# W1 times a fused matrix by Strassen: four pairs of seven block products, in a chain of conditional LoRA layers on one core

## The reference

```python
x = x + einsum('bct,bcd->bdt', x, L0_weights[adapter])            # C = 64, D = 64
x = x + x @ L1_W + (x @ L1_A[adapter]) @ L1_B[adapter]            # rank 16, 16 adapters
x = x + x @ L2_W.T + (x @ L2_A[labeler]) @ L2_B.T * 0.5           # rank 32, 5 labelers
x = x + x @ L3_W.T + 2.0 * top-2-gated sum over 8 experts of rank 16
```

## Time and profile before

| | us |
|---|---|
| median of 3 runs | 543.56 (542.45 to 544.06) |
| the profiled execution, its own time | 544.38 |
| its span | 542.6 |

### The profile page before, as it was taken

How to read it: one execution, slowest core, us unless ns; L and a number is a source line. 1 busy time by engine, 2 the same in 40 slices (tenths; PEclk the granted TensorE clock), 3 DMA queues, 4 the chain that set the end, 5 groups by cost and what they waited for, 6 DMA issues and landing times.

```text
span 542.6 us, 9086 instructions
## 1 busy us (share of the span) xinstructions
PE 533.7 (98%) x2812; PEld 475.9 (88%) x2812; DVE 252.5 (47%) x609; ACT 162.8 (30%) x314; POOL 155.9 (29%) x247
## 2 busy tenths in 40 slices
PE   7999999999999999999999999999999999999996
PEld 6999999999999999999987788888888888888885
DVE  3842222132211111213987675664756647566463
ACT  4641312121110111113734332333323333233322
POOL 2501000000000000353653644434444344443400
PEclk9999999999999999999999999999999999999999
DMA  7803020035242111120050421323313233132312
GB/s 280 291 32 132 2 78 16 1 106 170 83 152 76 40 39 44 39 82 1 23 167 2 132 98 48 102 80 123 104 46 103 79 120 107 43 105 79 118 29 77
DMA packets 24060, 46.76 MB, mean 86 GB/s; under 512 B 7636, under 2 KB 13396, under 8 KB 23908
## 3 DMA queue, kind: packets, MB, share of 16 engines
q1 hardware_dynamic: 23844, 45.85, 25.4%
q0 software_dynamic: 192, 0.59, 0.3%
HBM read 33.39 MB, written 13.04 MB: 86 GB/s over the span
## 4 chain that ended last, share of the span: by engine, by line
PE 95%; DVE 2%; DMA 1%; SPq 0%; ACT 0%; issue 0%; POOL 0%; DVEq 0%
PE bank L1281 27%; PE bank L1315 25%; PE bank L1232 15%; PE bank L1301 8%; PE bank L1363 4%; PE bank L1371 4%; PE bank L1248 4%; PE bank L1379 3%; PE bank L1366 1%; PE bank L1365 1%; DMA w2raw<-in_w_dram 1%; PE bank L1325 1%; DVE t_lo L902 1%; PE bank L1342 0%; PE bank L1352 0%; PE bank L1331 0%
## 5 line engine op out<-in xcount | busy, mean ns | idle before, releaser
L1281 PE MATMUL bank<-e_lo,w1t_hi 128*128 128x488 f32 (+2 forms) x240 | 86.9, 362 | 0.0
L1281 PE MATMUL bank<-e_hi,w1t_hi 128*128 128x488 f32 (+2 forms) x240 | 86.8, 362 | 0.0
L1281 PE MATMUL bank<-e_hi,w1t_lo 128*128 128x488 f32 (+2 forms) x240 | 86.7, 361 | 0.0
L902 DVE TENSOR_TENSOR w1t_lo<-raw,w1t_hi 128x1024 fp32r<-128x1024 f32 x18 | 24.7, 1370 | 76.6 <-ACT w1t_hi L661 60.0
L1232 PE MATMUL bank<-g_hi,w2s_hi 128*128 128x384 f32 (+1 forms) x144 | 48.3, 336 | 0.3 <-DVE e_lo L902 0.3
L1281 PEld LDWEIGHTS bank<-e_lo,w1t_hi 128*128 128x128 f32 x240 | 45.2, 188 | 3.9
L1281 PEld LDWEIGHTS bank<-e_hi,w1t_hi 128*128 128x128 f32 x240 | 45.0, 188 | 4.0
L1281 PEld LDWEIGHTS bank<-e_hi,w1t_lo 128*128 128x128 f32 x240 | 45.1, 188 | 3.9
L1232 PE MATMUL bank<-g_lo,w2s_hi 128*128 128x384 f32 (+1 forms) x144 | 48.2, 335 | 0.0
L1232 PE MATMUL bank<-g_hi,w2s_lo 128*128 128x384 f32 (+1 forms) x144 | 48.2, 335 | 0.0
L902 DVE TENSOR_TENSOR e_lo<-bank,e_hi 128x384 fp32r<-128x384 f32 (+1 forms) x24 | 13.0, 558 | 60.7 <-ACT e_hi L696 60.7
(11 more groups left out here) (233 smaller groups left out, 1330.0 us busy)
## 6 DMA issues: line engine op xcount, KB each, us to landing
raw<-in_x_dram SPq DMA_DIRECT2D x16, 512.0 KB, 3.6
out_dram<-ost SPq DMA_DIRECT2D x32, 256.0 KB, 2.1
b1s<-b1scr SPq DMA_DIRECT2D x32, 217.5 KB, 2.7
raw<-in_b1w_dram SPq DMA_DIRECT2D x10, 512.0 KB, 3.3
w2raw<-in_w_dram SPq DMA_DIRECT2D x7, 512.0 KB, 8.0
graw<-in_w3a3wr_dram SPq DMA_DIRECT2D x4, 768.0 KB, 8.7
graw<-in_w3a3wr_dram SPq DMA_DIRECT2D x8, 196.0 KB, 7.5
b1scr<-b1stage_hi SPq DMA_DIRECT2D x8, 192.0 KB
```

The costliest lines, as they stand in the source:

```text
L902: V.tensor_tensor(dst, src, f32(hi), ALU.subtract).then_inc(signal, 1)
L1281: ins = nc.tensor.matmul(stage_bank(u, j)[:, 0:WIDTH[c]], W1T[u][a][:, k, :], EX[c][z][:, k, :], start=(k == 0 and (a, z) == TERMS[0]), st ...
```

## The change

The W1 rows are multiplied by E with Strassen's scheme (the form with seven products, the same that the x tiles use). Row tile j and row tile j + 4 make a pair. Per pair PE runs seven products of 12 matmuls of 512 columns (`rows_pair`), and two products with the 296 extra columns (`row_tables`, 24 matmuls each). The LoRA rows stay plain, in chunks of 512, 512 and 296 columns. The combinations of E's four quarters, e1 to e4, are whole 128x2048 tiles. Since E is kept as high and low parts only, each takes several passes: e1 three and e2 two on DVE, e3 three and e4 two on POOL, during the LoRA rows. Then ACT and DVE split them (`e_hi`, `e_lo`). The left combinations of each pair are POOL's (`row_sum`, 128x512). M's own combinations, formed by POOL row by row before, become four instructions of 128x1536 on POOL (`front_sum`) late in and after the last pair, and four of 128x512 on DVE (`back_sum`). Nearly every buffer moves.

The order on PE:

```diff
-            pe.wait_ge(s_a2l, 2)
-            for r in range(2 + LORA):
-                rows(r, r % 2)
-            with pe.Fori(1 + LORA // 2, ROWS // 2) as i:
-                rows(2 * i, 0)
-                rows(2 * i + 1, 1)
+            def row_tables(j, h):
+                e = 2 * j + h
+                above(pe, s_rxa, 2 * (e - 1))
+                left = XR if h else XA
+                pe.wait_ge(s_rl, OPS * j + OPERAND["xb" if h else "xa"])
+                for k in range(K):
+                    for a, z in TERMS:
+                        ins = nc.tensor.matmul(bank[RT + h][:, 0:EC], left[a][:, k, :], EM[z][:, k, EXT], ...)
+            def rows_pair(j):
+                ops = OPS * j
+                if j:
+                    pe.wait_ge(s_ra, 2 * j - 1)
+                else:
+                    pe.wait_ge(s_accl, ACC_A + 3)
+                row_product("p1")
+                pe.wait_ge(s_rl, ops + OPERAND["cs"])
...
+                row_product("p5")
+                pe.wait_ge(s_rl, ops + OPERAND["ds"])
...
+                row_product("p6")
+                row_tables(j, 1)
+                pe.wait_ge(s_rcp, 2 * j + 1)
+                row_product("p2")
+                pe.wait_ge(s_radd, 3 * j + 2)
+                pe.wait_ge(s_rl, ops + OPERAND["cs2"])
+                row_product("p7")
+                pe.wait_ge(s_rl, ops + OPERAND["xb2"])
+                row_product("p3")
+                pe.wait_ge(s_radd, 3 * j + 3)
...
+                row_product("p4")
+                if j < LASTR:
+                    row_tables(j + 1, 0)
+            pe.wait_ge(s_a2l, 1)
+            for r in range(LORA):
+                lora_rows(r)
+            row_tables(0, 0)
+            for j in range(NR):
+                rows_pair(j)
```

DVE's list from the end of stage 1:

```diff
+            w1_lo(1)
+            dve.wait_ge(s_accl, ACC_A - 1)
+            V.tensor_tensor(e1, e_part("b12", 0), e_part("b11", 0), ALU.subtract).then_inc(s_e1, 1)
+            dve.wait_ge(s_e1, 1)
+            V.tensor_tensor(e1, e1, e_part("b12", 1), ALU.add).then_inc(s_e1, 1)
+            dve.wait_ge(s_e1, 2)
+            V.tensor_tensor(e1, e1, e_part("b11", 1), ALU.subtract).then_inc(s_e1, 1)
+            identity_rows(0, 0)
+            identity_rows(0, 1)
+            lora_lo(0, 0)
+            dve.wait_ge(s_e1, 3)
+            V.tensor_tensor(e2, e_part("b22", 0), e1, ALU.subtract).then_inc(s_e2, 1)
+            lora_lo(0, 1)
+            dve.wait_ge(s_e2, 1)
+            V.tensor_tensor(e2, e2, e_part("b22", 1), ALU.add).then_inc(s_e2, 1)
+            lora_lo(0, 2)
+            dve.wait_ge(s_e2, 2)
+            e_lo(1)
+            row_lo(XA[1][:, :, :], raw[0][:, :, :], XA[0][:, :, :], OPERAND["xa"])
+            lora_lo(1, 0)
+            e_lo(3)
+            lora_lo(1, 1)
+            row_lo(CS[1], tmp[:, :, :], CS[0], OPERAND["cs"])
+            dve.wait_ge(s_e4, 1)
+            e_lo(2)
+            lora_lo(1, 2)
```

DVE in each pair, and with `j == LASTR` in the last one (`row_lo` splits a left operand):

```diff
+            def rows_pair_lo(j):
...
+                row_lo(DS[1], tmp[:, :, :], DS[0], ops + OPERAND["ds"])
+                row_lo(XR[1][:, :, :], raw[1][:, :, :], XR[0][:, :, :], ops + OPERAND["xb"])
+                if j == LASTR:
+                    split_lo("b11", FRONT)
...
+                V.tensor_tensor(bank[BB][:, :], bank[BB][:, :], held_p1[:, :], ALU.add).then_inc(s_radd, 1)
+                row_lo(CS[1], raw[1][:, 0:KH, :], CS[0], ops + OPERAND["cs2"])
...
+                V.tensor_tensor(bank[BD_][:, :], bank[BB][:, :], held_p5[:, :], ALU.add).then_inc(s_radd, 1)
+                row_lo(XR[1][:, 0:KH, :], tmp[:, :, :], XR[0][:, 0:KH, :], ops + OPERAND["xb2"])
...
+                if j == LASTR:
+                    split_lo("b12", FRONT)
+                    dve.wait_ge(s_s0h, 1)
+                    lo(S[1][:, :, 0:C3], TBC[:, :, :], S[0][:, :, 0:C3], s_s0l)
+                    split_lo("b21", FRONT)
+                dve.wait_ge(s_rw, made + PRODUCT["p7"])
+                V.tensor_tensor(m_row(j, "b22"), bank[BB][:, :], held_p5[:, :], ALU.add).then_inc(s_radd, 1)
```

DVE in the first pair of x tiles:

```diff
+                dve.wait_ge(s_ra, 2 * NR)
+                split_lo("b21", BACK)
+                split_lo("b22", FRONT)
+                dve.wait_ge(s_ml, SPLIT_LO["b12b"])
+                back_sum("t1")
+                split_lo("b22", BACK)
+                dve.wait_ge(s_tb, FORMED["t1"])
+                back_sum("t3")
+                plain_lo(CS[1], raw[1][:, 0:KH, :], CS[0], 2)
+                plain_lo(DS[1], raw[1][:, KH:K, :], DS[0], 3)
+                dve.wait_ge(s_ml, SPLIT_LO["b22b"])
+                dve.wait_ge(s_tb, FORMED["t3"])
+                back_sum("t2")
                 V.memset(f32(h1c[:, :]), 0.0).then_inc(s_z, 1)
+                dve.wait_ge(s_tb, FORMED["t2"])
+                back_sum("t4")
                 xn_lo(0, YB)
```

POOL's list from the end of stage 1:

```diff
+            e3, e4, e2 = (TF[n][:, :, :] for n in (2, 3, 1))
+            pool.wait_ge(s_accl, ACC_A - 1)
+            nc.gpsimd.tensor_tensor(e3, e_part("b22", 0), e_part("b12", 0), ALU.subtract).then_inc(s_e3, 1)
+            pool.wait_ge(s_e3, 1)
+            nc.gpsimd.tensor_tensor(e3, e3, e_part("b22", 1), ALU.add).then_inc(s_e3, 1)
+            pool.wait_ge(s_e3, 2)
+            nc.gpsimd.tensor_tensor(e3, e3, e_part("b12", 1), ALU.subtract).then_inc(s_e3, 1)
...
+            row_sum(0, "s1")
+            pool.wait_ge(s_e2, 2)
+            nc.gpsimd.tensor_tensor(e4, e_part("b21", 0), e2, ALU.subtract).then_inc(s_e4, 1)
+            pool.wait_ge(s_e4, 1)
+            nc.gpsimd.tensor_tensor(e4, e4, e_part("b21", 1), ALU.add).then_inc(s_e4, 1)
+            for j in range(NR):
+                if j:
+                    row_sum(j, "s1")
+                for which in ("s2", "s3", "s4"):
+                    row_sum(j, which)
...
+            front_sum("t1")
+            pool.wait_ge(s_tf, FORMED["t1"])
+            pool.wait_ge(s_ml, SPLIT_LO["b12f"])
+            front_sum("t3")
             pool.wait_ge(s_idx, 48)
+            pool.wait_ge(s_s0l, 1)
+            for s in range(2):
+                nc.gpsimd.memset(bdraw[s], 0.0).then_inc(s_bdz, 1)
+            pool.wait_ge(s_rxa, 4 * NR)
+            pool.wait_ge(s_a1, 16)
+            take(0, choose(0))
...
             pool.wait_ge(s_bdz, 2)
+            diagonal(0, 0, 0)
+            pool.wait_ge(s_tf, FORMED["t3"])
+            pool.wait_ge(s_ml, SPLIT_LO["b22f"])
+            front_sum("t2")
+            diagonal(1, 1, 0)
+            pool.wait_ge(s_tf, FORMED["t2"])
+            front_sum("t4")
             take(1, choose(1))
```

More of the change, by code:

```diff
@@ L106, in cond_resid_kernel @@
[L106 to L112, removed]
@@ new lines, in cond_resid_kernel, with raw_front, raw_back @@
+    raw = [at(f"raw{n}", [P, K, P], F32, RAW0 + 4096 * n) for n in range(2)]
+    tmp = at("tmp", [P, KH, P], F32, TMP0)
+    TBC = at("tbc", [P, K, C3], F32, TBC0)
+    KF = KH - 1
+    MRF = at("mr", [P, KF, 2, 2, BANK], F32, Z0)
+    MLF = at("ml", [P, KF, 2, 2, BANK], F32R, Z0)
+    QUARTER = dict(b11=(0, 0), b12=(0, 1), b21=(1, 0), b22=(1, 1), t1=(0, 0), t3=(0, 1), t2=(1, 1), t4=(1, 0))
+    def raw_front(name):
+        h, c = QUARTER[name]
+        return MRF[:, :, h, c, :]
+    def raw_back(name):
+        h, c = QUARTER[name]
+        return EF[1][:, 2 * h + c, RIGHT_COLS]
@@ L1142, in first_pair_lo @@
[L1142 to L1148 removed]
+                for j in range(NR):
+                    rows_pair_lo(j)
@@ L1286, in _, with row_tables @@
-            for r in range(2 + LORA):
-                rows(r, r % 2)
-            with pe.Fori(1 + LORA // 2, ROWS // 2) as i:
-                rows(2 * i, 0)
-                rows(2 * i + 1, 1)
+            def row_tables(j, h):
+                e = 2 * j + h
[4 more added lines that the diff above has]
+                    for a, z in TERMS:
+                        ins = nc.tensor.matmul(bank[RT + h][:, 0:EC], left[a][:, k, :], EM[z][:, k, EXT], start=(k == 0 and (a, z) == TERMS[0]),
+                                               stop=(k == K - 1 and (a, z) == TERMS[-1]), skip_group_check=True)
+                ins.then_inc(s_rx, 1)
@@ new lines, in _, with row_product @@
+            ROW_LEFT = dict(p1=(XA, 0), p5=(CS, 0), p6=(DS, 0), p2=(XA, KH), p7=(CS, 0), p3=(XR, 0), p4=(XR, KH))
+            RIGHT = dict(p1="b11", p5="t1", p6="t2", p2="b21", p7="t3", p3="b22", p4="t4")
+            TO = dict(p1=BA, p5=BC, p6=BB, p2=BA, p7=BB, p3=BD_, p4=BB)
+            OPENS = ("p1", "p5", "p6")
+            def row_product(name):
+                (left, k0), right, to = ROW_LEFT[name], RIGHT[name], bank[TO[name]]
+                for n in range(3 * KH):
+                    k, (a, z) = n // 3, TERMS[n % 3]
+                    ins = nc.tensor.matmul(to[:, :], left[a][:, k0 + k, :], e_right(right, z, k), start=(name in OPENS and n == 0),
+                                           stop=(n == 3 * KH - 1), skip_group_check=True)
+                ins.then_inc(s_rw, 1)
@@ L1305, in _ @@
```

(2 more changed lines are left out.)

784 lines of the change are left out of this document (437 added, 347 removed).

## The result

The changed kernel takes 562.93 us (median of 4 runs, 562.13 to 566.53), the kernel before 543.19 beside it: a ratio of 1.038, 95% interval 1.033 to 1.042. It is slower by 3.8%; the forecast was 559.4 us, 549 to 568.

A forecast was written before the change was run, and what follows sets the result against it. PE, busy 98% of the span, was taken as the bound. Gain -11.7, LoRA wait +13.1, last pair and first x pair +11.4, restarts +3.0 sum to +15.8: 560.2, or 559.4 us on the median's scale, range 549 to 568.

The forecast's parts named there:

- Strict turns on memory: DVE and POOL memory-to-memory instructions alternate, one whole instruction each; DVE's 2048-column e1 passes take about 6.6 us instead of 2.3.
- The rival that long instructions don't hold DVE: POOL's 4.6 us passes run beside DVE's, so only the gain is left: 531.1 us on the median's scale; chance 0.07.
- The two variants of arbitration: Rivals on who gets the port: DVE first whenever it asks, 556 us, chance 0.15; POOL first, 564 us, chance 0.10.
- the second variant: POOL goes first whenever both ask: waits of 13.6, 3.4, 3.0 and 10.7 us, time 564 us; chance 0.10.
- POOL's prices: POOL's long instructions, from its rows at 128 and 512 columns: 4.6 us at 2048 columns, 3.5 at 1536.
- The LoRA wait: After the LoRA rows, PE waits 13.1 us at `row_tables(0, 0)` for XA's low part, behind e4's second pass.
- The last pair's wait: In the last row pair, PE waits 3.4 us before p4 for its sum, behind front sums and splits.
- The first x pair's wait: PE waits 8.1 us before `mixed(0, 0)` for `xn_lo(0)`, with eight DVE instructions ahead, each letting one of POOL's in.
- The small wait at a low rank step: In the first x pair, behind the mixed product: a wait of 0.5 us at `h2_across(1, 1)`.
- The list of PE: W1 rows: 115.1 us of matmuls become 103.4, a gain of 11.7, with 296-column matmuls interpolated at 0.1384 us.
- Restarts: PE's slower pace after the 13 and 8 us waits: 1.5 us each, 3.0 in all, 0 as the other end.
- The 1.3 us row of before: In the kernel before, six matmuls after a 1.3 us wait take 1.15 us, read as no loss.

The follow-up runs named there:

- experiment 2: Changed kernel with POOL's five E passes replaced by two memsets and its four front sums cut to 16 columns: 535.0 us.
- experiment 4: Changed kernel with each of POOL's five 128x2048 E passes cut into four 128x512 instructions, nothing left out: 562.17 us.
- experiment 5: Changed kernel with all ten E passes on DVE, ordered by when PE needs the results, nothing left out: 548.9 us, ratio 1.0085 to the kernel before.
- experiment 6: Kernel of experiment 2 with DVE repeating the sum behind p7 four times in the second row pair and seven in the third, making p4 wait: 541.57 us.
- exp. 8: Same instructions as exp. 7, with the splits and sums of the t's spread over the first x pair: 540.35 us, ratio 0.9937 to the kernel before.
- exp. 7: Experiment 5 plus three of the four front sums moved from POOL to DVE, behind the low rank steps: 544.13 us, ratio 1.0014 to the kernel before.
- exp. 1: Changed kernel with POOL's five 128x2048 E passes left out, two memsets in their place: 548.49 us.

## Why the prediction was right

The forecast was 559.4 and the time 562.9, inside the range, by the mechanism that carried the forecast: the list of PE gets shorter, and three new waits that come of the turns between DVE and POOL cost more than it gains. Point by point:

- **Strict turns on memory.** Right for the long passes, and at the sizes that no row of before had shown: DVE's e1 passes at 6.70 and 6.59 (said: about 6.6), POOL's third at 6.55 (6.7). The rival that long instructions don't hold DVE (531) describes the kernel of experiment 2, 535.0. The two variants of arbitration made waits of 2.2 and 6.6 before p5 and p6, or of 13.6, 3.4, 3.0 and 10.7; the trace has 13.4, 3.2 and 6.6 and none before p5 or p6. By time alone the second variant (564) was nearer to the 562.9 than the forecast; it is the 6.6 in place of 10.7 that speaks against it. "Strict" is too strong: POOL and not DVE had the first turn, which changed the sum little, and experiments 4 and 5 have exceptions.
- **POOL's prices.** 4.6 us at 2048 columns and 3.5 at 1536, drawn through its rows at 128 and 512: measured 4.63 and 3.50. The 4497 ns that the Trainium skill, "GPSIMD Engine Reference", section "3. Performance versus the Vector engine", gives is 0.13 short of the uncontended 4.63.
- **The LoRA wait.** 13.1 predicted, 13.4 measured; its exit by e4's second pass as written.
- **The last pair's wait.** 3.4 predicted, 3.2 measured.
- **The first x pair's wait.** 8.1 predicted, 6.6 measured. The step said that eight instructions of DVE would each let one of POOL's in. Its timeline shows t2 and t4 taking their turns, but the three of the first diagonal ran at 271.4 to 272.8, mostly while DVE read PSUM or waited for ACT, and `take` began only at 285.2: fewer of POOL's were in DVE's way than counted. The small wait at a low rank step, 0.5 in the forecast, is 0.9.
- **The list of PE.** The gain of 11.7 was too large by 1.0 in the pairs and by 0.8 behind them. A row pair takes 26.06 instead of 25.8: a 512-column matmul 8.38 / 36 = 0.2328 in the chain instead of 0.2285, a 296-column one 3.28 / 24 = 0.1367, near the interpolated 0.1384. The interpolation held; the 0.2285, from the first x pair's row, did not carry over, and the later x pairs of the kernel before would have given the higher value (ten matmuls in 2.32 us at 305.74). And in the later x pairs, said to cost nothing, each takes 0.13 more (34.14 instead of 34.01). No run here undoes that; all the kernels with Strassen rows have it. It stays open.
- **Restarts.** This is the term with the largest share of the error. Two of 1.5 were taken, 3.0; measured are three, 5.5: 5.55 - 3.28 = 2.3 behind the 13.4 us, 1.8 behind the 3.2 us, for which the sum had nothing, and 1.4 behind the 6.6 us. The 1.3 us row of before was taken as a sign that short waits cost nothing, and a wait of 3.2 counted as short. Experiment 6 shows that a wait of this length is enough to bring such a loss. Experiment 4 shows that it need not: there the same wait cost 0.1, in experiment 5 it cost 2.75. So the term was wrong in its size, and no single size would have been right.

The errors have both signs: rows 3.7 us dearer than the sum (pairs 1.0, restarts 2.6, waits 0.1), first x pair 1.4 cheaper (its wait 1.5, its restart 0.1 and the 0.2 before it cheaper, the small wait 0.4 dearer), the start 1.1 cheaper, the rest 0.8 dearer. That makes 2.0 us between the profiled executions, and it is in part luck that it is no more. The other 1.5 us of the miss are the choice of the executions: the profiled one of the kernel before lay 0.8 above its median, that of the changed kernel 0.8 below.

## What to carry to other kernels

Where two engines work from memory to memory at once, add their work up as if it were one engine's, in the order of the turns, and give long passes to the one that does them faster: here DVE took five passes of POOL's over and the operand that TensorE waited for came 19.8 us earlier, counted from the start of the rows. A DVE instruction that reads PSUM doesn't take part (0.69 us beside POOL). Cutting the instructions smaller moves the waiting from one engine to the other, and short instructions beside long ones pay most.

A wait of TensorE of 2 us and more can cost more than itself: nothing on top in two of the cases below, 1.4 to 2.75 us in the others. Count each wait that a schedule brings in newly with about 2 us more, and put 0 and 3 as the bounds of that term. The kernel that removes the wait gains this too.

An average (POOL busy 36%, DVE 57%) shows none of this; the timeline of the two engines side by side, read by the ends of their instructions, does.

## What the runs showed of the hardware

What TensorE loses behind a wait (us of the first product after it, against the same product elsewhere; by the chains, and by the starts of matmuls in the two rows of experiment 4 with 0.1):

| wait | first product | later | loss |
|---|---|---|---|
| 0.9 (exp. 6) | 3.02 + 3.45 | 2.75 + 3.29 | 0.4 |
| 2.3 (exp. 8) | 4.58 | 2.74 | 1.8 |
| 2.8 (exp. 4) | 3.39 | 3.28 | 0.1 |
| 2.9 (exp. 7) | 4.52 | 2.74 | 1.8 |
| 3.1 (exp. 6) | 4.61 | 2.75 | 1.9 |
| 3.2 (exp. 4) | 2.87 | 2.75 | 0.1 |
| 3.2 (exp. 1) | 4.47 | 2.75 | 1.7 |
| 3.2 (changed kernel) | 4.57 | 2.75 | 1.8 |
| 3.2 (exp. 5) | 5.50 | 2.75 | 2.75 |
| 6.6 (changed kernel) | 0.96 + 2.43 | 0.58 + 1.39 | 1.4 |
| 9.2 (exp. 4) | 4.90 | 2.75 | 2.1 |
| 13.4 (changed kernel) | 5.55 | 3.28 | 2.3 |

From 2.3 us on, the loss doesn't follow the length of the wait: the same wait before the same product, 3.2 us before the last p4, cost 0.1, 1.7, 1.8 and 2.75 us in four kernels. What makes the difference no run here shows. Behind the waits that cost 1.4 us and more the granted clock stands at 0.50 for a while. Behind the 0.9 us of experiment 6 it stays at 1.00, so the 0.4 is no matter of the clock. Stretches of the changed kernel (window, its length, busy time of PE, PEld, DVE, ACT and POOL with counts, granted clock, DMA's share, GB/s), with the LoRA wait in the first the 3.2 us wait in the third, most of the 6.6 us one in the fourth, and nothing unusual in the second:

```profile
146.00:165.00 19.00, 5.71 (x26) 5.66 (x27) 19.00 (x9) 5.02 (x5) 12.63 (x3) 0.64 0.34 115
165.00:244.00 79.00, 79.00 (x401) 67.68 (x400) 28.20 (x39) 25.35 (x46) 17.10 (x13) 1.00 0.16 59
244.00:270.00 26.00, 22.81 (x101) 18.57 (x100) 20.50 (x14) 13.63 (x18) 16.27 (x12) 0.93 0.22 83
270.00:286.00 16.00, 10.47 (x58) 8.70 (x56) 14.31 (x11) 6.35 (x9) 13.20 (x15) 0.92 0.58 184
```

A value between 0.50 and 1.00 is a mean over a stretch that holds both levels, 1.2 and 2.4 GHz. In smaller windows of the same trace the clock is 1.00 at 147 to 150 us, in the beginning of the LoRA wait, 0.50 from 155 to 163, and 1.00 again from 164 on; the 296-column matmuls start 0.25 us apart in the slow part and 0.137 apart behind it. In experiment 4 it is 1.00 throughout the wait from 263 to 266 us and behind it. The half pace behind the waits agrees with the rule that the prediction cited from the Trainium skill, "TensorE: Matmul & The Clock Gate", section "What's actually happening". The clock's row of before shows its top even in the opening, where the transposes ran at half their later pace. Either the row misses a slow stretch there or those transposes are slow for another reason. In both cases the row was no proof that a restart costs nothing.
